# Lookup gather: asks past the last node leave the gather through its bounds check, and VectorE fills their rows

## The reference

```python
r_input = jax.random.randint(jax.random.fold_in(_rk, 1), (512, 200), 78, 199964, jnp.int32)
...
h1 = gcn_conv(emb, W1, b1, row, col, NTOKEN)
lookup = gcn_conv(h1, W2, b2, row, col, NTOKEN)
return lookup[input]
```

## Time and profile before

| | us |
|---|---|
| median of 3 runs | 7286.15 (7277.15 to 7286.85) |
| the profiled execution's own time | 7271.66 |
| its span | 7269.9 |
| POOL busy in the span | 4662.6 (64%) |
| DVE busy | 4445.4 (61%) |
| PE busy | 4020.8 (55%) |

### The profile page before, as it was taken

One profiled execution on the slowest core, in us unless ns is written; L12 is line 12 of the kernel. 1 busy time (PEld: TensorE's weight loads), 2 busy tenths in 40 slices (PEclk: granted clock), 3 DMA queues, 4 the chain that ended last, 5 costly groups with the idle time before them and its releaser, 6 DMA issues.

```text
span 7269.9 us, 202878 instructions
## 1 busy us (share of the span) xinstructions
PE 4020.8 (55%) x60793; PEld 3053.1 (42%) x60794; DVE 4445.4 (61%) x12751; ACT 2005.4 (28%) x5160; POOL 4662.6 (64%) x4819
## 2 busy tenths in 40 slices
PE   8977787888888888553455556546556550000000
PEld 5633454555555556543445555446445450000000
DVE  8988898999999998547455656556556551000000
ACT  0037777777777776323000000000000000000000
POOL 0013577777777777774777777777777756776661
PEclk9989999999999999666666767667667675555555
DMA  0001111111111111111211111111111117999998
GB/s 15 0 21 50 37 38 38 40 38 39 39 38 39 39 38 40 39 39 51 51 39 39 39 39 39 39 39 40 39 39 39 39 29 63 40 43 43 43 43 49
DMA packets 167796, 282.10 MB, mean 39 GB/s; under 512 B 79372, under 2 KB 79382, under 8 KB 167120
## 3 DMA queue, kind: packets, MB, share of 16 engines
q0 software_dynamic: 151040, 219.19, 27.2%
q1 hardware_dynamic: 12832, 54.72, 1.9%
q10 hardware_dynamic: 3760, 6.16, 0.3%
HBM read 227.84 MB, written 51.92 MB: 38 GB/s over the span
## 4 chain that ended last, share of the span: by engine, by line
POOL 39%; issue 23%; PE 16%; DVE 10%; DMA 7%; DVEq 2%; ACT 0%; POOLq 0%; SPq 0%; ACTq 0%
POOL scratch L394 29%; POOL acc L429 10%; PE ps L562 8%; PE ps L634 7%; DMA scratch<-table,source 7%; DVE acc L996 3%; DVE late L975 2%; DVE late L986 2%; DVE place_i L953 1%; PE ps L687 1%; DVEq L994 0%; DVE picked L947 0%; DVEq L986 0%; DVE acc L280 0%; POOL scratch L388 0%
## 5 line engine op out<-in xcount | busy, mean ns | idle before, releaser
L394 POOL DMA_INDIRECT scratch<-table,source x3920 | 3753.8, 958 | 1272.5 <-issue 1148.1
L634 PE MATMUL ps<-scratch,late 128*128 x52800 | 2749.1, 214 | 1499.2 <-DMA scratch<-table,source 1369.2
L634 PEld LDWEIGHTS ps<-scratch,late 128*128 128x128 f16 x52800 | 2490.2, 111 | 2016.0 <-issue 1774.0
L996 DVE TENSOR_TENSOR acc<-acc,ps 128x256 f32 x4400 | 1817.2, 413 | 1277.6 <-PE ps L634 1243.6
L986 DVE TENSOR_SCALAR late<-ramp,target 128x512 f16<-128x512 f16 x3850 | 1381.0, 359 | 109.8 <-PE ps L634 85.1
L486 ACT ACTIVATE late<-prt_onehot,scratch 125x128 f16<-125x128 f16 x4000 | 1217.3, 387 | 453.5 <-DVE prt_onehot L809 353.0
L562 PE MATMUL ps<-late 125*128 125x440 f16 x4000 | 1067.9, 357 | 235.0 <-DVE late L975 222.9
L429 POOL DMA_INDIRECT acc<-lookup,ask_i x800 | 755.6, 945 | 361.3 <-issue 338.0
L975 DVE TENSOR_SCALAR late<-ramp,tcol 125x440 f16<-125x440 f16 x2000 | 714.4, 364 | 0.0
L497 ACT ACTIVATE late<-distance,one_col 128x512 f16<-128x512 f16 x550 | 397.0, 722 | 525.4 <-PE ps L634 488.5
L363 POOL CAST scratch<-acc 128x896 bf16 (+1 forms) x14 | 15.2, 1088 | 679.3 <-DVE acc L1075 679.3
(11 more groups left out here) (128 smaller groups left out, 1029.9 us busy)
## 6 DMA issues: line engine op xcount, KB each, us to landing
scratch<-table,source POOLq DMA_INDIRECT x3920
out<-acc SPq DMA_DIRECT2D x40, 640.0 KB, 58.8
table<-scratch SPq DMA_DIRECT2D x28, 672.0 KB, 3.4
acc<-lookup,ask_i POOLq DMA_INDIRECT x800, 117.5
lookup<-acc SPq DMA_DIRECT2D x4, 1568.0 KB, 5.1
late<-embT ACTq DMA_DIRECT2D x47, 128.0 KB, 2.6
scratch<-edge_index SPq DMA_DIRECT2D x2, 976.6 KB
ask_i<-r_input SPq DMA_DIRECT2D x1, 400.0 KB, 16.8
```

Source lines behind the costliest of these rows:

```text
L394: pool.indirect_dma_start(out=place, out_offset=None, in_=table[r], in_offset=bass.IndirectOffsetOnAxis(ap=source[:, t:t + 1], axis=0)).th ...
L634: last = pe.matmul(visit_ps[k][:, n * FEAT:(n + 1) * FEAT], target_onehot[:, k, n * P:(n + 1) * P], row[:, part * FEAT:(part + 1) * FEAT], ...
L996: dve.tensor_tensor(dst, dst, visit_ps[k].rearrange("p (n f) -> p n f", f=FEAT), ALU.add).then_inc(visits_added, 1)
```

## The change

Asks at or past node 25,000 get an index that is larger than the last row of the table: `find_asked` has two more DVE instructions for it. The gather has a bound, and entries above it move nothing. So that the right row stands in those places, SP loads the row of node 24,999 into all partitions of a new tensor `last_row` once `lookup` is written, and DVE copies it 20 times beside each other into a slot before POOL gathers into it. POOL waits for DVE (`slots_filled`), where it waited for `out_written`; that wait is DVE's now.

```diff
+        last_row = sb("last_row", [P, FEAT], F32)
...
+            lp, lt = (NODES - 1) % P, (NODES - 1) // P
+            sp.wait_ge(lookup_written, 16 * 4)
+            sp.dma_start(last_row[:, :], lookup[lp * NT + lt:lp * NT + lt + 1, :].broadcast_to([P, FEAT])).then_inc(last_loaded, 16)
...
             for u in range(OUT_GROUPS):
                 i, h = divmod(u, OUT_SLOTS)
-                if i > 0:
-                    pool.wait_ge(out_written[h], 16 * i)
+                pool.wait_ge(slots_filled, u + 1)
                 pool.sem_inc(waits_passed, 1)
                 for k in range(OUT_GROUP):
                     t = u * OUT_GROUP + k
                     pool.indirect_dma_start(
                         out=out_rows[:, h, k, :], out_offset=None, in_=lookup,
-                        in_offset=bass.IndirectOffsetOnAxis(ap=ask_i[:, t:t + 1], axis=0)).then_inc(rows_fetched[h], 16)
+                        in_offset=bass.IndirectOffsetOnAxis(ap=ask_i[:, t:t + 1], axis=0),
+                        bounds_check=P * NT - 1, oob_is_err=False).then_inc(rows_fetched[h], 16)
...
+                last = (NODES - 1) % P * NT + (NODES - 1) // P
+                step(dve.tensor_scalar(ask_f, ask_f, float(NODES), float(P * NT - last), ALU.is_ge, ALU.mult))
+                step(dve.tensor_tensor(ask_i[:, :], ask_i[:, :], ask_f, ALU.add))
...
+            dve.wait_ge(last_loaded, 16)
+            for u in range(OUT_GROUPS):
+                i, h = divmod(u, OUT_SLOTS)
+                if i > 0:
+                    dve.wait_ge(out_written[h], 16 * i)
+                dve.tensor_copy(out_rows[:, h, :, :], last_row[:, :].unsqueeze(1).broadcast_to([P, OUT_GROUP, FEAT])).then_inc(slots_filled, 1)
```

More of the change, by code:

```diff
@@ L253, in build @@
         lookup_written = sem("lookup_written")
+        last_loaded = sem("last_loaded")
+        slots_filled = sem("slots_filled")
         rows_fetched = [sem(f"rows_fetched{h}") for h in range(OUT_SLOTS)]
@@ L1177 @@
 BASE_STEPS = 1 + CHUNKS + 6 + CHUNKS + 3 + 3 + 4 + 1 + CHUNKS // 2 + 3
-ASK_STEPS = 6
+ASK_STEPS = 8
 def kernel(**inputs):
```

## The result

| | us |
|---|---|
| before | 7286.5 (7277.15 to 7289.51, 4 runs) |
| with the change | 7103.48 (7100.12 to 7108.65, 4 runs) |
| ratio | 0.9752, 95% interval 0.9735 to 0.9768 |
| span of the profiled execution | 7100.5 |

The change makes the kernel 183 us faster. The forecast was 7079, with a range of 7035 to 7275.

A forecast was written before the change was run, and what follows sets the result against it. The DMA engines were taken to bound the last stage, with POOL's pace the floor just below. Stalls -94.7, tail -135.1, start +5.0 and fills +18 sum to -206.8, so 7286.15 becomes 7079 us, range 7035 to 7275.

The forecast's parts named there:

- stalls: Last stage: POOL's waits of 4 to 7 us at every 20th gather from the 474th disappear, -94.7 us.
- tail: Program end: the 142.9 us from POOL's last gather to the end shrink to 7.8, -135.1 us.
- bound on POOL: Last-stage gathers: the index bounds check was taken to cost POOL 0; possible ends were +756 and -661 us.
- start: Before POOL's first last-stage gather: waiting for the last_row load and first fill, +5.0 us (4.3 to 6.3).
- fills beside gathers: Last stage: 40 DVE fills of 0.83 us slow POOL's gathers by 0.55 of their length, +18 us (0 to 33).
- likeliest case: Last stage at POOL's own pace, 7079 us, 7060 to 7097 by the unknown terms; chance 0.64.
- case 2: Last-stage gathers: the check lengthens each by less than the gain; 7176 us with 0.12 us, anything 7100 to 7270; chance 0.13.
- The prediction's own sign: Profile after: a mean gather outside 0.94 to 0.98 us makes the forecast wrong by 800 times the difference.
- The bound of the stage: Last stage: DMA engines set the pace before, 30.9 us per 20 gathers; POOL does after, 25 us.
- Skipped entries: Last-stage gathers: entries past the bound move nothing, so a packet has one row, not 8: 0.17 us instead of 1.34.
- rival 4: Last stage: skipped entries still travel to or from a dummy place, packets stay at 1.34 us, 7291 us; chance 0.08.
- rival 5: Last stage: gathers get shorter, making 16 entries, not 128; 6701 us with half saved, 7040 with little; chance 0.09.

## Why the prediction was right

The sum again, with what the stages of the traces measured:

| term | predicted | measured |
|---|---|---|
| stalls | -94.7 | -94.7 |
| tail | -135.1 | -133.4 |
| bound on POOL | 0 | +41.5 |
| start | +5.0 | +4.1 |
| fills beside gathers | +18 | +3.5 |
| sum | -206.8 | -179.0 |

By the medians it is -183. The forecast was right by its range, and less so by its reasons: its likeliest case (chance 0.64, 7060 to 7097) did not come. What came is case 2, to which it gave 0.13, at the lower edge of its 7100 to 7270: the check makes each gather longer, but by less than the gain. The prediction's own sign for this was there, a mean of the gather outside 0.94 to 0.98: 1.000, for which it gave 800 x 0.055 = 44 us more.

- *The bound of the stage.* Right: DMA engines before, POOL after. That the pace follows from 7 of 8 reads going to one row was an inference and is now shown twice, by taking the row away (7056 us) and by sending everything to it (+150 us).
- *Skipped entries.* Right in effect, off in size and kind. I had 0.17 us a packet, by rows that move; it is 0.035, since a packet's 1.34 us was waiting for the row and not the moving of 8 rows. And it is not so that entries above the bound move nothing: they do travel, as rival 4 had it, but as 4 bytes each and without the wait, so that the rival's time did not come. Where those 4 bytes come from and go to, no run shows.
- *The bounds check.* This is the term that was mis-sized: 0 taken, 0.052 us a gather measured, 41.5 us in all. The argument that one comparison more costs nothing beside 0.945 us did not hold. It lay between my value and the 0.121 of the smallest index operation, and the range reached beyond. Skipping itself adds nothing and saves nothing on POOL, so rival 5 falls too.
- *The start* came as worked out: the load landed 3.0 us after its issue, the fill took 0.83 us. With eight fills back to back the first three gathers took 1.43, 1.19 and 1.19 us.
- *The fills' length* was right (834 ns for 826); the price beside gathers was five times too high, 18 us for 3.5. 0.55 of a fill was read from `decode`, where DVE ran one such instruction behind the other. A single fill catches a gather once, and in this kernel at a phase that costs 0 to 0.19 us. That phase is luck: in the kernel that skips all, most fills come just ahead of a gather and cost about 0.6 us each, and there the fills cost 16.7 us in all, close to the 18. The rate of the earlier trace rows is real; what the prediction lacked is the phase, which no row of it could give. The lock for the whole fill that the Trainium skill describes ("SBUF — State Buffer", section "Who interferes with whom") would be 33 us; neither case here shows it in full, 0.64 of 0.83 us is the nearest.
- *The tail:* the last gather lands after 2.3 us and not 3.0, but from the last write's issue to the end it is 7.2 us and not 4.3 (7093.3 to 7100.5). The write lands as fast as before (2.9 us for 3.0). What is longer is SP's wait for PE's sequencer at the program's close, 3.9 us where it was 1.0. It is 3.7 to 4.0 in the three kernels of the first session in which POOL works to the end, and 1.1 in the one in which it is done 144 us before; why, the runs do not tell.

```profile
SPq L70 <- PEq L70: 3.9, 1, 3.9
```

Before:

```profile
SPq L70 <- PEq L70: 1.0, 1, 1.0
```

- *`find_asked`* hid as expected: the two instructions take 1.57 us and two hand-overs, and DVE's wait for PE behind them is 11.85 us where it was 13.22.

The bound's term, put at nothing, and the fills' term, put too high by 14.5 us, had opposite signs. So the sum came out 24 us off by the medians, where it would have been 38 with the fills right; that is luck.

## What to carry to other kernels

Look at which rows a gather reads, not only at how many: here one DRAM row gave a read each 13.6 to 13.8 ns, and as soon as POOL asked for more than that, the whole queue ran at that row's pace. Two copies of the row were enough. Skipping by a bound is another way, at 0.052 us a gather on POOL. Which of them is better was decided by something outside the kernel: copies by 42 us at first (39 within one session, against the kernel with the bound and no fills), skipping by 61 us in a later session, so both should be timed together more than once.

## What the runs showed of the hardware that I had not expected

- An entry skipped by the bound still moves 4 bytes in its packet (3600 packets, 0.13 MB), and the packets are as many as before.
- The gather with a bound takes POOL 0.052 us more, whether none, 7 of 8 or all entries are skipped (0.997 us in the median each time).
- The number of gathers in flight at which POOL is held is one and the same: 113, counted by whole groups landed. It is so whether the first hold comes at the 474th gather (before), the 574th (bound alone) or the 394th (all asks in one row).
- A float32 copy of 0.83 us on DVE costs a gather beside it between 0 and 0.64 us, by its phase.
- In the later sessions gathers that move all their rows took no less than 1.40 us a step on average from about the 190th on (the 245th with a bound), and the passes took 2900 us longer. Both are unexplained.
